# Experts in tiles of 256 rows, first weights stationary, and the context product on VectorE

## The reference, cut to what matters

```python
x = x + attention(layernorm(x))          # 16 heads of 16, bias by relative position, softmax
h = layernorm(x)
sh = gelu(h @ sw1 + sb1) @ sw2 + sb2     # shared expert, for every token
logits = h @ gate_w.T + expert_bias      # 7 routed experts
topv, topi = top_k(logits, 2); w = softmax(topv)
routed = sum over the two chosen e of w_e * (gelu(h @ rw1[e] + rb1[e]) @ rw2[e] + rb2[e])
x = x + sh + routed
```

## Time and profile before

| what | value |
|---|---|
| median of 3 runs | 1011.3 us |
| the profiled execution's time | 1011.57 us |
| its span, first to last instruction | 1009.8 us |
| busy over the span: PE, PEld, DVE, ACT, POOL | 817.5, 580.7, 673.5, 461.6, 289.7 us |
| mean granted TensorE clock | 0.895 of 2.4 GHz |
| PE's largest idle before the expert stage's up products (L1509) | 21.6 us |
| share of the span on the chain that ended last, by PE L1509 | 7% |

### The profile page before, as it was taken

The page is one execution under the profiler, slowest core; times in us unless marked ns, Lnnn a source line. Parts: engine busy times, 40 slices in busy tenths (PEclk is TensorE's granted clock), DMA queues, the critical chain, the costliest instruction groups (busy, mean ns, idle before and its releaser), DMA issues. The chain is left out here.

```text
span 1009.8 us, 20238 instructions
## 1 busy us (share of the span) xinstructions
PE 817.5 (81%) x6409; PEld 580.7 (58%) x6409; DVE 673.5 (67%) x2033; ACT 461.6 (46%) x730; POOL 289.7 (29%) x430
## 2 busy tenths in 40 slices
PE   5799699999999999999992466666448888888872
PEld 3688366666666666666652355555237666666651
DVE  5565578888888888888813456767635555555544
ACT  2344036666666666666663344444313333333220
POOL 2111011111111111111104456666552333333300
PEclk9999669999999999999996678888558999999965
DMA  4998945445543553333527223333232333333268
GB/s 115 297 329 301 245 104 142 125 113 132 156 124 107 145 147 102 106 102 99 160 81 227 92 99 111 123 116 105 63 136 85 95 89 93 96 95 96 69 219 291
DMA packets 92257, 139.58 MB, mean 138 GB/s; under 512 B 14952, under 2 KB 61312, under 8 KB 91982
## 3 DMA queue, kind: packets, MB, share of 16 engines
q1 hardware_dynamic: 82146, 118.09, 39.3%
q0 software_dynamic: 9840, 19.67, 5.9%
q10 hardware_dynamic: 172, 0.56, 0.2%
HBM read 84.27 MB, written 54.28 MB: 137 GB/s over the span
## 5 line engine op out<-in xcount | busy, mean ns | idle before, releaser
L687 DVE CUSTOM_DVE_ANT_0 sums<-pS,near 128x512 bf16<-128x512 f32 x512 | 329.2, 687 | 53.2 <-PE pS L747 45.0
L718 ACT ACTIVATE prob<-pE 128x1024 f32<-128x1024 f32 x256 | 248.5, 1022 | 153.5 <-PE pE L772 153.5
L772 PEld LDWEIGHTS pE<-bandT,place 64*128 64x128 f32 x2048 | 167.5, 190 | 12.3
L772 PE MATMUL pE<-bandT,place 64*128 64x244 f32 (+2 forms) x2048 | 164.8, 272 | 0.0
L747 PE MATMUL pS<-k_st,q_st 48*128 48x512 f32 x512 | 140.2, 478 | 11.0 <-DVEq L673 7.2
L786 PE MATMUL pC<-prob,v_aug 128*32 128x512 f32 x1024 | 135.8, 604 | 1.0 <-ACT ctx_sb L726 1.0
L747 PEld LDWEIGHTS pS<-k_st,q_st 48*128 48x128 f32 x512 | 64.2, 194 | 120.7 <-DVE nmax L687 87.0
L764 PE MATMUL pE<-q_st,k_st 62*128 62x512 f32 x512 | 115.6, 405 | 0.5 <-DMA q_st<-negated_maxima 0.5
L1039 POOL DMA_INDIRECT expert_rows<-rb,xr x70 | 67.1, 959 | 142.8 <-DVE rb L1224 139.9
L1363 ACT ACTIVATE cn<-cn 128x256 f32<-128x256 f32 x70 | 29.2, 417 | 131.1 <-DVE cn L1232 131.1
L1509 PE MATMUL pU<-w1p,cT 128*128 x420 | 70.8, 305 | 21.6 <-DVE cT L1214 20.2
(11 more groups left out here) (166 smaller groups left out, 1124.4 us busy)
## 6 DMA issues: line engine op xcount, KB each, us to landing
xr<-routed_rows SPq DMA_DIRECT2D x70, 129.0 KB, 2.2
q_parts<-qk SPq DMA_DIRECT2D x16, 512.0 KB, 4.8
k_parts<-qk SPq DMA_DIRECT2D x16, 512.0 KB, 4.7
q_st<-q_parts SPq DMA_DIRECT2D x64, 128.0 KB, 2.8
k_st<-k_parts SPq DMA_DIRECT2D x64, 128.0 KB, 2.9
ctx<-ctx_sb SPq DMA_DIRECT2D x32, 256.0 KB, 2.8
xr<-expert_rows SPq DMA_DIRECT2D x16, 512.0 KB, 5.8
near<-bias_by_distance SPq DMA_DIRECT2D x16, 448.0 KB, 5.1
```

The costliest lines, as they stand in the source:

```text
L687: dve.tensor_tensor_reduce(sums[:, r % 4], pS[:, unit % PS], near[:, hg % 2, j, lead:lead + S], -1.0, BIG, ALU.add, ALU.min, nmax[:, j, t: ...
L718: act.activation(prob[:, par, 2 * step:2 * step + 2], pE[:, 2 * (step % 2):2 * (step % 2) + 2], ACT.Exp).then_inc(exp_done, 1)
L772: ins = pe.matmul(pE[:, bank + side, a:z], place[rows, half], bandT[rows, (quad // 2) % 2, pair, part, lead:lead + z - a], start=False, st ...
```

## The change

Two things are changed in `finish`, and the numbers that go with them.

**The context on VectorE.** `context` and its low part leave GpSimd's list and stand in VectorE's, the product behind `lows(i + 1)`, the low part behind the two `weights_lo`. The addition of the gate's bias goes from VectorE to ScalarE. GpSimd scatters half a batch later (`scatter(i - 1, 1)`, `scatter(i, 0)`), from three instead of two buffers. The pads are written by 7 DMAs of SP with a fetched address, not by GpSimd.

**Tiles of 256 rows.** A tile has 256 rows, two to a partition, and there are 38 (`NT`). The up product has the expert's first weights standing (copied for each tile to `w1c`, high part by ScalarE, low part by VectorE) and 256 rows moving, so its result has hidden units on the partitions: the bias is ScalarE's in the Gelu, and hidden rows are not turned. The Gelu is taken twice, in float32 and as the high part. The order on TensorE in step k is: up k+2, turn tile k+3, down k. Experts are fetched four at once (`NG`). Expert rows lie in DRAM so that a partition's four rows of a batch are next to each other.

```diff
-NT = 2 * B * S // P + NR - 1
+TS = 2 * P
+NT = (2 * B * S + NR * (TS - 1)) // TS
+NG = 4
...
+        w1c = x2T[:, XB - 1].rearrange("p c a s -> p (c a s)").rearrange("p (k z n) -> p k z n", k=2, z=2)
...
+        def up_bank(i, m):
+            return (pU[:, m] if i % 2 == 0 else pX[:, 1, m])[:, 0:TS]
...
@@ SP @@
+                sp.wait_ge(s["pads_done"], 1)
+                for e in range(NR):
+                    row = sp.value_load(pad_at[0:1, e:e + 1], min_val=0, max_val=NE * RS - TS)
+                    sp.dma_start(xs_dram[bass.ds(row, TS), :], g["pad_rows"][e]).then_inc(pad_out[0], 16)
                 sp.wait_ge(s["tab_done"], 2)
...
-                        rows = yc_dram[c * YR + b * S:c * YR + b * S + S].rearrange("(t p) d -> p t d", p=P)
+                        rows = yc_dram[c * YR + b * S:c * YR + b * S + S].rearrange("(p t) d -> p t d", p=P)
...
@@ GpSimd @@
-                context(0)
                 inverse_deviation(0)
-                context(1)
                 for i in range(B):
                     if i + 1 < B:
                         inverse_deviation(i + 1)
-                    if i + 2 < B:
-                        context(i + 2)
-                    scatter(i)
...
+                    if i >= 1:
+                        scatter(i - 1, 1)
+                    scatter(i, 0)
+                scatter(B - 1, 1)
...
@@ VectorE @@
+                def context(b):
+                    dve.wait_ge(g["cn_ld"], 16 * 2 * MC * (b + 1))
+                    dve.tensor_tensor(cn[:], cn[:], rb[:], ALU.mult).then_inc(s["c_ready"], 1)
+
+                def context_lo(b):
+                    for c in range(MC):
+                        dve.wait_ge(s["c_hi"], 2 * b + c + 1)
+                        dve.tensor_tensor(cT[:, 1, c], cn[:, c], cT[:, 0, c], ALU.subtract).then_inc(s["c_lo"], 1)
...
+                def weights_copy(i, expert):
+                    if i >= 2:
+                        dve.wait_ge(s["up_mm"], 2 * (i - 1))
...
+                    dve.tensor_copy(w1c[:, i % 2, 1], w1p[:, bass.ds(expert, 1), 1].rearrange("p a c n -> p (a c n)")
+                                    ).then_inc(s["wc_lo"], 1)
...
+                for k in range(-3, NT):
+                    if k + 3 < NT:
+                        if (k + 3) % NG == 0:
+                            experts = experts_of((k + 3) // NG)
+                        weights_copy(k + 3, experts[(k + 3) % NG])
+                        x_low(k + 3)
                     if k >= 0:
                         evict(k)
-                    if 0 <= k + 3 < NT:
-                        if k + 3 == 0:
-                            dve.wait_ge(s["b1_ld"], 16)
-                        bias(k + 3)
+                    if 0 <= k + 2 < NT:
+                        h_low(k + 2)
...
@@ ScalarE @@
+                def gelu(i, expert):
+                    for m in range(2):
+                        act.wait_ge(s["up_mm"], 2 * i + m + 1)
+                        if i >= 2:
+                            act.wait_ge(s["hlo"], i - 1)
+                            act.wait_ge(s["dn_mm"], 2 * (i - 1))
+                        bias = b1s[:, bass.ds(expert, 1), m]
+                        cols = slice(TS * m, TS * m + TS)
+                        act.activation(h_f[:, i % 2, cols], up_bank(i, m), ACT.Gelu, bias=bias)
+                        act.activation(hT[:, i % 2, 0, cols], up_bank(i, m), ACT.Gelu, bias=bias).then_inc(s["hhi"], 1)
...
+                        x_high(k + 3)
+                        weights_copy(k + 3, experts[k + 3])
+                    if 0 <= k + 2 < NT:
+                        gelu(k + 2, experts[k + 2])
...
@@ TensorE @@
+                def expert_up(i):
+                    pe.wait_ge(s["xlo"], i + 1)
+                    pe.wait_ge(s["wc_hi"], i + 1)
+                    pe.wait_ge(s["wc_lo"], i + 1)
                     if i >= 2:
...
+                        pe.wait_ge(s["hhi"], 2 * (i - 1))
+                    for m in range(2):
+                        for k, (c, (a, z)) in enumerate((c, hl) for c in range(MC) for hl in HL):
+                            ins = pe.matmul(up_bank(i, m),
+                                            w1c[:, i % 2, z, HID * c + P * m:HID * c + P * m + P],
+                                            xgT[:, i % 2, a, TS * c:TS * c + TS], start=k == 0, stop=k == 5)
+                        ins.then_inc(s["up_mm"], 1)
...
+                for k in range(-3, NT):
+                    if 0 <= k + 2 < NT:
+                        expert_up(k + 2)
+                    if k + 3 < NT:
+                        turn_tile(k + 3)
                     if k >= 0:
-                        expert_down(k)
-                    if 0 <= k + 3 < NT:
-                        expert_up(k + 3)
+                        if k % NG == 0:
+                            experts = experts_of(k // NG)
+                        expert_down(k, experts[k % NG])
```

More of the change, by code:

```diff
@@ L863, in finish @@
         slot_i = sb("slot_i", [P, B, 2, TT], I32)
-        pad = sb("pad", [P, NR, XW], F32)
-        pad_i = sb("pad_i", [P, NE], I32)
-        over = sb("over", [P, NE, S // 16], F32)
+        pad_at = sb("pad_at", [1, NE], I32)
+        over = sb("over", [P, NE, STEPS], F32)
         tiles_of = sb("tiles_of", [P, NE], F32)
@@ L1008, in inverse_deviation, with scatter @@
                     pool.tensor_scalar(nbias[:], nbias[:], -1.0, None, ALU.mult).then_inc(s["rstd2d"], 1)
[L1010 removed]
+                def scatter(b, c):
                     if b == 0:
@@ L1216, in h_low, with experts_of @@
+                def experts_of(k):
+                    return nc.values_load_multi_w_load_instructions(
+                        table[0:1, 1, NG * k:NG * k + NG], engines=[dve.engine], min_val=0, max_val=NE - 1)[1]
                 def h_low(i):
-                    dve.wait_ge(s["hhi"], i + 1)
-                    dve.tensor_tensor(hT[:, i % 2, 1], pX[:, 1, i % 2, 0:HID], hT[:, i % 2, 0], ALU.subtract).then_inc(s["hlo"], 1)
+                    dve.wait_ge(s["hhi"], 2 * i + 2)
+                    dve.tensor_tensor(hT[:, i % 2, 1], h_f[:, i % 2], hT[:, i % 2, 0], ALU.subtract).then_inc(s["hlo"], 1)
@@ L1220, in evict @@
                 def evict(i):
[L1221 removed]
                     if i >= NY:
[L1223 to L1233 removed]
+                        dve.wait_ge(y_out[(i - NY) % NXG], 32 * ((i - NY) // NXG + 1))
@@ L1235, in gather_add @@
+                    for t in range(2):
+                        dve.wait_ge(s["dn_mm"], 2 * i + t + 1)
+                        dve.tensor_scalar(y_rows(i)[:, t], pD[:, t, i % 2], xg[:, i % NXG, t, D + 1:D + 2], None,
+                                          ALU.mult).then_inc(s["ev_done"], 1)
                 def gather_add(b):
@@ L1255, in _ @@
                 dve.reciprocal(den[:], den[:]).then_inc(s["den_inv"], 1)
+                context(1)
+                context_lo(1)
                 lows(0)
@@ L1269, in _ @@
                         lows(i + 1)
+                    if i + 2 < B:
+                        context(i + 2)
                     slots(i)
@@ L1513, in expert_down @@
-                def expert_down(i):
-                    expert = pe.value_load(table[0:1, 1, i:i + 1], min_val=0, max_val=NE - 1)
-                    pe.wait_ge(s["hlo"], i + 1)
-                    if i >= 2:
-                        pe.wait_ge(s["ev_done"], i - 1)
-                    for k, (m, (a, z)) in enumerate((m, hl) for m in range(2) for hl in HL):
-                        ins = pe.matmul(pD[:, i % 2, 0], hT[:, i % 2, a, P * m:P * m + P],
-                                        w2p[:, bass.ds(expert, 1), z, m].rearrange("p a n -> p (a n)"), start=k == 0, stop=k == 5)
-                    ins.then_inc(s["dn_mm"], 1)
+                        pe.wait_ge(s["hhi"], 2 * (i - 1))
@@ new lines, in expert_up, with expert_down @@
+                    for m in range(2):
[4 more added lines that the diff above has]
+                        ins.then_inc(s["up_mm"], 1)
+                def expert_down(i, expert):
+                    pe.wait_ge(s["hlo"], i + 1)
+                    for t in range(2):
+                        if i >= 1:
+                            pe.wait_ge(s["ev_done"], 2 * (i - 1) + t + 1)
+                        for k, (m, (a, z)) in enumerate((m, hl) for m in range(2) for hl in HL):
+                            ins = pe.matmul(pD[:, t, i % 2], hT[:, i % 2, a, TS * m + P * t:TS * m + P * t + P],
+                                            w2p[:, bass.ds(expert, 1), z, m].rearrange("p a n -> p (a n)"),
+                                            start=k == 0, stop=k == 5)
+                        ins.then_inc(s["dn_mm"], 1)
@@ L1523, in _, with experts_of @@
+                def experts_of(k):
+                    return nc.values_load_multi_w_load_instructions(
+                        table[0:1, 1, NG * k:NG * k + NG], engines=[pe.engine], min_val=0, max_val=NE - 1)[1]
                 pe.wait_ge(s["small_lo"], 5)
```

254 lines of the change are left out of this document (107 added, 147 removed).

## The result

The changed kernel takes 960.8 us (median of 4 runs, 958.5 to 965.0) against 1010.8 us; the ratio is 0.951, with a 95% interval of 0.948 to 0.955. It is faster, by 50 us. The profiled execution took 960.4 us, its span is 958.5 us, so 51.3 us of span have gone.

| stretch | before | after | difference |
|---|---|---|---|
| start to the attention's end (`wo_p` on ScalarE) | 530.9 | 527.8 | -3.1 |
| from there to the last output projection's start | 169.6 | 174.7 | +5.1 |
| last output projection to the experts' first turn | 55.0 | 48.7 | -6.3 |
| first turn to last scatter (the expert stage) | 203.6 | 157.3 | **-46.3** |
| last scatter to the end | 50.7 | 50.0 | -0.7 |

The account below looks back on a forecast made before the run. The prediction took TensorE's products, turns and expert fetches to bound the expert stage. Span 1009.8 less 7 before the experts, 43 in their stage and 3 at the end gives 956.8, with 1.8 outside 958.6, forecast 958 us; range 948 to 975.

Parts of the forecast that it names:

- So this stage is bound by TensorE's own sequencer.: Expert stage before: per 128 rows, 2.0 us of products and turns plus 0.87 us fetching expert numbers on TensorE.
- Period 4.0, stage 160.: Changed expert stage: 3.65 us plus 0.4 for fetches per 256-row tile, rounded to 4.0; 160 us instead of 203.6.
- The fetch terms.: Every fourth expert tile: 0.95 us more on TensorE, 0.65 on VectorE and ScalarE; together 0.4 us per tile.
- the sign to look for: Expert stage: up products 3.6 us apart, 4.3 to 4.5 where TensorE fetches; its weight loads idle near 12 us on "issue".
- No slack on VectorE and ScalarE.: Expert tiles: VectorE's weight copy ends just when the next x subtraction is due, at 6.3 us; 0.05 us added.
- Before the experts, gain 7.: Context part and pads before the experts: first turn at 748.5 instead of 755.50 us; bounds 2 and 12.
- The rounds: Context part: context on VectorE makes a batch's round 0.75 us later than 23.86; six rounds cost 4.5 us.
- The last stretch, gain 3.: Last scatter to the end: expert rows read 4 KB a piece instead of 1 KB shorten waits; bounds nothing and 8 us.
- The rule weighed: Expert stage: VectorE's fp32 SBUF copies share ports with GpSimd, so weight copies and scatters would hold each other up.
- rival 2: Expert stage: weight copy waits for a scatter, costing 31 us, 989 us; chance 0.12 together with other lateness.
- Rival 1: Expert stage: TensorE runs at its own 3.4 to 3.6 us, fetches issued ahead; 15 us less, 943; chance 0.13.
- Rival 3: Expert stage: down products cover nothing, so the kernel is slower; from a 5.6 us period, 1018 us at 5.8; chance 0.02.

Follow-up runs that it names:

- `NG = 1`: Changed kernel with each engine fetching one expert number per tile instead of four at once, at the same place: 962.4 us.
- the kernel of 934 us: Changed kernel with single fetches, VectorE's and ScalarE's put later where they wait, and TensorE's order turns, down, up: 934.4 us, ratio 0.924.

## Why the prediction came out right

958 us was forecast, and 960.8 was measured. The sum was right to 3 us, and part of that is luck: the expert stage won 3 us more than forecast (46.3 against 43), and the two other parts 5 us less (5.0 against 10). One of its reasons was not right.

- **"So this stage is bound by TensorE's own sequencer."** This failed. Without TensorE's fetches the tile of 128 rows takes 2.55 us, not the 2.0 of TensorE's own work, and grouping TensorE's fetches alone gives nothing. The waits on "issue" named what came last, and another wait stood 0.3 us behind it (21.8 us over 70 tiles, of the 0.87 waited). The prediction wrote that the waits name no engine; but its own name VectorE's low part (L1214) ahead of both up products, with 0.30 and 0.29 us. That was the sign of the second wait. The sum did not need this step: the new period was worked out from the new kernel's own parts.
- **Where the 46.3 us come from** (stage lengths): before, 203.6; without TensorE's fetches 181.8. Changed, 157.3; without fetches 146.9. So the larger tile with its shorter circle (no bias step, no turned hidden rows) is worth 181.8 - 146.9 = 34.9, and the fetches, 21.8 before and 10.4 after, 11.4. Three things limit this split. The 146.9 are nearer 145, as said above, which moves under 2 us from the fetches to the tile. VectorE's 70 fetches are still in the 181.8, and none is in the 146.9, so some of the 34.9 may be theirs (VectorE waited 12.5 us on them). And no run parts the 256 rows from the shorter circle.
- **Period 4.0, stage 160.** Measured 3.87 (3 x 3.54 + 4.85, over 4) and 157.3. The plain tile was put at 3.65. The turns' copies do stand behind TensorE's own rate, as the prediction said, and by more than it thought: TensorE alone makes 3.25 where 3.4 was forecast, and the order costs 0.3 where it was 0.2 and 0.05.
- **The fetch terms.** 0.95 on TensorE and 0.65 on VectorE and ScalarE, in each fourth tile, were forecast. It is 0 and 1.3. The sum, 1.6, was near by luck; the place was wrong, and with it the sign to look for (long tiles "where TensorE fetches"; its weight loads wait 2.6 us on "issue", not 12).
- **No slack on VectorE and ScalarE.** Not so in plain tiles: VectorE waits 1.1 us in each. The single fetch fits in there, which took 11.9 us off the stage and 14 off the kernel.
- **Before the experts, gain 7.** Measured 4.3, of which 3.1 are the attention's chance, so the change itself won 1.2. The first two batches won 2.7 (3.5 forecast). The last part won 6.3. The rounds lost 7.8 over seven, where 4.5 over six was forecast: about 4.5 of it is the lower clock level in two rounds, which the prediction did not have, and an undisturbed round takes 24.1 to 24.3 where it said 24.6. That the pads are the last to arrive was right; the first load comes at 748.4, not near 746.
- **The last stretch, gain 3.** Measured 0.7. The load of 512 KB lands in 4.7 us in place of 5.8, but VectorE waits again for the loads of the last batches, against the earlier trace rows:

```profile
xr<-expert_rows SPq DMA_DIRECT2D x16, 512.0 KB, 4.7
...
947.65 1.22 DVE L1240 TENSOR_TENSOR x1c<-x1c,xr 128x1024 f32<-128x1024 f32 x1 [2.35 <-DMA xr<-expert_rows]
952.64 1.23 DVE L1240 TENSOR_TENSOR x1c<-x1c,xr 128x1024 f32<-128x1024 f32 x1 [2.51 <-DMA xr<-expert_rows]
```

- **The rule weighed, and rival 2.** The rule of the Trainium skill (SBUF — State Buffer, Who interferes with whom), by which whoever comes second is blocked, agrees with the trace. But what holds the scatter here is VectorE's subtraction (L1226), not the new weight copy (L1217) that the prediction named. GpSimd's scatters beside VectorE's work, in two tiles of the changed kernel:

```profile
852.63 0.96 POOL L1032 DMA_INDIRECT expert_rows<-cn,xr  x1 [1.31 <-DVE cn L1233]
853.83 0.69 DVE L1226 TENSOR_TENSOR h_p<-ctx_sb,h_p 128x512 fp32r<-128x512 f32 x1 [1.09 <-ACT h_p L1385]
853.89 1.47 POOL L1032 DMA_INDIRECT expert_rows<-cn,xr  x1 [0.30 <-issue]
854.44 0.42 DVE L1217 CAST x2T<-w1p 128x512 fp32r x1
...
864.55 0.96 POOL L1032 DMA_INDIRECT expert_rows<-rb,xr  x1 [2.63 <-DVE rb L1233]
864.59 0.69 DVE L1226 TENSOR_TENSOR h_p<-ctx_sb,h_p 128x512 fp32r<-128x512 f32 x1
865.20 0.54 DVE L1217 CAST x2T<-w1p 128x512 fp32r x1
```

The scatter that began 0.06 us behind the subtraction took 1.47 us in place of 0.96; the one that began 0.04 ahead of it took 0.96. The later in the subtraction it begins, the less it is held: 1.28 us at 0.24 behind (with `NG = 1`), 1.18 at 0.34 and 0.96 at 0.57 behind (in the kernel of 934 us). The copy does not lengthen it: in the last case the two ran together and the copy took 0.42. Behind a scatter that began first the copy took 0.54. GpSimd still waits about 1 us for VectorE in each tile, so nothing waits for it, and rival 2, which put 0.9 us on VectorE in nearly every tile, did not come.
- **Rival 1** (943 us, TensorE at its own rate) is what the kernel of 934 us reaches, with single late fetches and the other order, which the change does not have. Rival 3, the slower side, was far off: the down products cover all but 0.3 us of the copies.

## What to carry to other kernels

Before a wait is priced, ask how far behind it the next one stands: leave the suspected cost out once, and only what then goes was its price (22 us here, of 61 waited). Leave it out on every engine that pays it: here VectorE's share was left in, and its price stayed unknown. A short fixed cost on an engine that sets a pace belongs in the gap where that engine waits, in pieces that fit it; grouping makes it cheaper in sum and dearer in the one tile that has to hold it. And an order is judged with its neighbours: the same order of turns, down and up products was the slowest of the changed kernel's variants with the fetch in the wrong place and the fastest with it in the right one.

## What the runs showed of the hardware that was not expected

- A fetch of an expert number into registers took 0.52 us on VectorE (0.31 load, 0.19 and 0.02 behind it), one of four 1.36 us, with the load alone at 0.52; one of four on ScalarE took 0.98. On TensorE a fetch was free behind some 2 us of queued matmuls.
- On one of the chips the kernel before took 1050.8 us, and 1011.8 and 1012.0 on two others. The four variants of the changed kernel there took 959 to 975 us. Each of their profiles holds an operation that came 3 to 9 us late with no engine named. The kernel before was not profiled there, so whether such waits make up the 39 us stays open.
- A scatter of GpSimd that began 0.06 us behind VectorE's subtraction of 128x512 took 1.47 us in place of 0.96, and one that began 0.04 us ahead of it took 0.96. VectorE's copy of 128x512 beside a scatter took 0.42 us, or 0.54 when the scatter was first.
- The granted clock fell to its lower level inside some rounds of the same instructions and not in others (mean 0.76 against 0.85 over a round), at 2.4 us for a round.
